# A mixture-of-experts kernel on one core: a finer table for the written order of its pieces, and a third buffer for sorted rows

## The reference

```
h = layernorm(x + o, g1, b1)
probs = softmax(h @ wg); topv, topi = top_k(probs, 2)
h1 = gelu(einsum('bsd,edf->ebsf', h, w1) + bb1)
y = einsum('ebsf,efd->ebsd', h1, w2) + bb2
moe = einsum('ebsd,bse->bsd', y, w)
return layernorm(h + moe, g2, b2)
```

## Time and profile before

| | |
|---|---|
| runs (3) | 1172.96, 1174.55, 1190.9 us; median 1174.55 |
| profiled execution, first to last instruction (its span) | 1192.8 us |
| its own time | not recorded beside the span; the span is 1.9 us above the longest of the three runs |
| instructions | 29724 |
| granted TensorE clock, mean | 0.898 |
| HBM traffic | 145.1 MB read, 38.7 MB written |

### The profile page before, as it was taken

One profiled execution on the slowest core, in us unless ns is written; L12 is line 12 of the kernel. 1 busy time (PEld: TensorE's weight loads), 2 busy tenths in 40 slices (PEclk: granted clock), 3 DMA queues, 4 the chain that ended last, 5 costly groups with the idle time before them and its releaser, 6 DMA issues. The chain is left out here.

```text
span 1192.8 us, 29724 instructions
## 1 busy us (share of the span) xinstructions
PE 1022.4 (86%) x10913; PEld 818.6 (69%) x10913; DVE 680.8 (57%) x2458; ACT 670.5 (56%) x1494; POOL 572.7 (48%) x693
## 2 busy tenths in 40 slices
PE   4799979998989989999989989998999988866470
PEld 2566656886877867686777867687777866766470
DVE  5657665655558835686568835686556723520314
ACT  1243424875758756675667757576666756534240
POOL 2223356235465455555565455554464456542515
PEclk9988877998999989898999979799999979887795
DMA  3394105555555545555556545555556545676562
GB/s 71 86 193 109 37 19 162 167 164 181 154 160 150 172 138 156 147 154 172 149 154 171 165 137 144 153 158 154 160 163 176 170 137 164 202 244 221 212 194 51
DMA packets 117239, 181.01 MB, mean 152 GB/s; under 512 B 13128, under 2 KB 80232, under 8 KB 117096
## 3 DMA queue, kind: packets, MB, share of 16 engines
q1 hardware_dynamic: 108904, 162.32, 47.7%
q0 software_dynamic: 8192, 16.79, 4.9%
HBM read 145.10 MB, written 38.68 MB: 154 GB/s over the span
## 5 line engine op out<-in xcount | busy, mean ns | idle before, releaser
L1173 POOL TENSOR_SCALAR_AFFINE_SELECT probs<-probs 128x512 f32<-128x512 f32 x256 | 182.5, 721 | 262.1 <-ACT probs L706 257.1
L706 ACT ACTIVATE probs<-ps_quad 128x768 f32<-128x768 f32 x256 | 193.7, 807 | 150.3 <-PE ps_quad L527 87.8
L744 ACT ACTIVATE act<-ps_ring,weights 128x128 f32<-128x128 f32 x696 | 191.8, 387 | 96.4 <-PE ps_ring L623 48.0
L874 DVE TENSOR_REDUCE shift_cols<-ps_quad 128x2 f32<-128x512 f32 (+3 forms) x256 | 149.9, 586 | 139.8 <-PE ps_quad L508 125.6
L632 PE MATMUL ps_ring<-weights,act 128*128 128x128 f32 x1392 | 190.8, 285 | 31.1 <-issue 16.4
L632 PEld LDWEIGHTS ps_ring<-weights,act 128*128 128x128 f32 x1392 | 174.5, 198 | 35.1 <-issue 21.6
L623 PE MATMUL ps_ring<-tile_t,weights 128*128 128x128 f32 x1392 | 187.6, 292 | 3.9 <-issue 3.2
L623 PEld LDWEIGHTS ps_ring<-tile_t,weights 128*128 128x128 f32 x1392 | 174.0, 204 | 16.8 <-issue 13.2
L1236 POOL DMA_INDIRECT picked<-sorted_outputs,place x128 | 123.7, 966 | 79.8 <-issue 78.6
L999 DVE TENSOR_TENSOR tile_y<-ps_ring,weights 128x128 f32<-128x128 f32 x174 | 48.8, 287 | 182.2 <-PE ps_ring L632 101.2
L1222 POOL DMA_INDIRECT sorted_rows<-h_rows,place x128 | 124.5, 972 | 53.5 <-issue 34.6
(11 more groups left out here) (165 smaller groups left out, 1531.5 us busy)
## 6 DMA issues: line engine op xcount, KB each, us to landing
weights<-expert_weights SPq DMA_DIRECT2D x174, 578.0 KB
tile_rows<-sorted_rows SPq DMA_DIRECT2D x56, 192.0 KB
sorted_outputs<-tile_y SPq DMA_DIRECT2D x56, 192.0 KB
query_key_parts<-qk SPq DMA_DIRECT2D x32, 256.0 KB, 5.0
k<-query_key_parts SPq DMA_DIRECT2D x64, 64.0 KB
q<-query_key_parts SPq DMA_DIRECT2D x64, 64.0 KB
sorted_rows<-zeros SPq DMA_DIRECT2D x2, 1472.0 KB, 10.7
xs<-in_L_attn_x SPq DMA_DIRECT2D x32, 64.0 KB, 2.3
```

Source lines behind the costliest of these rows:

```text
L706: sc.activation(probs[:, r % PROBS, 2 * a:2 * a + 2, :], ps_quad[:, 2 * a:2 * a + 2, 0:3 * P], ACT.Exp, scale=HD ** -0.5).then_inc(pair_fr ...
L744: ins = sc.activation(act[:, k % ACTS, f, :], bank(use)[:, f * P:(f + 1) * P], ACT.Gelu_apprx_tanh, bias=weights_of(k)[:, 2 * F + f:2 * F ...
L874: dve.tensor_reduce(shift_cols[:, late, groups], ps_quad[:, groups, 0:split], AX.X, ALU.max)
L1173: pool.affine_select(out=both, in_=both, compare_op=ALU.is_ge, fill=0.0, base=0, pattern=[[0, 2], [0, 2], [1, P]], channel_multiplier=-1). ...
```

## The change

1. `PLACES` holds a number for each kind of piece, for each of five stretches (set 0, set 1, sets 2 to 5, set 6, set 7) and, inside a set, for each turn (each sequence, job, row tile, batch or tile of the set). The numbers differ from the old ones mostly by tenths.
2. Sizes of sets may differ (`SET_SIZES`); all are 2, as before. Where sizes were constants there are functions now.
3. `DEPTH = 3`: three `sorted_rows`, `sorted_outputs`, `place` and `expert_at`, used in turn, with the waits for set s - 3 in place of s - 2, and three fills with zeros.

```diff
+SET_SIZES = (2, 2, 2, 2, 2, 2, 2, 2)
+DEPTH = 3
...
-    "scatter2": 12.578, "scatter3": 13.235, "load_tiles0": 13.754, "load_tiles": 12.816, "load_weights0": 13.277,
...
+    "exps0": ((0.263, 0.148, 0.021, 0.477), (0.283, 0.255, 0.363, 0.234), (0.399, 0.227, 0.334, 0.381),
+        (0.473, 0.228, 0.368, 0.356), (0.372, 0.24, 0.356, 0.169)),
...
+    "exps3": ((1.629, 1.758, 1.929, 2.013), (1.882, 1.617, 1.81, 1.881), (1.674, 1.722, 1.567, 1.822),
+        (1.834, 1.821, 1.794, 1.82), (1.826, 1.985, 1.818, 1.765)),
...
+    "scatter": ((12.159, 12.25, 12.394, 12.445, 12.758, 12.945, 13.288, 13.718),
+        (12.044, 12.325, 12.421, 12.604, 12.976, 13.002, 13.228, 13.358),
+        (11.675, 12.302, 12.614, 12.652, 12.931, 13.159, 13.355, 13.536),
+        (11.827, 12.226, 12.231, 12.665, 12.833, 13.182, 13.5, 13.582),
+        (11.087, 11.272, 11.391, 11.668, 12.614, 12.979, 13.089, 13.611)),
...
+def stretch_of(s):
+    return {0: 0, 1: 1, SETS - 2: 3, SETS - 1: 4}.get(s, 2)
...
-        for t in range(SET_TT):
-            put(8 * s, f"scatter{t // 2}", "scatter", s, t)
+        for t in range(SET_SIZES[s] * TT):
+            put(at, "scatter", "scatter", s, t)
...
+    def place(half, name, piece):
+        return half + PLACES[name][stretch_of(set_of(piece))][turn_of(piece)]
...
-                for i in range(2):
+                for i in range(DEPTH):
                     sp.dma_start(sorted_h[i].rearrange("(t p) d -> p t d", p=P),
                                  zeros[:, :].unsqueeze(1).broadcast_to([P, TILES, D])).then_inc(zeroed, 16)
...
-                if s >= 2:
-                    dve.wait_ge(combined, 2 * (s - 1))
...
+                if s >= DEPTH:
+                    dve.wait_ge(combined, FIRST_JOB[s - DEPTH + 1])
...
-                if s >= 2 and t == 0:
+                if s >= DEPTH and t == 0:
                     for par in range(2):
-                        pool.wait_ge(tile_y_out[par], 16 * (BATCHES // 2) * (s - 1))
...
+                        pool.wait_ge(tile_y_out[par], batches_stored(s - DEPTH, par))
```

More of the change, by code:

```diff
@@ L76, with set_of, turn_of @@
 }
+BY_SEQUENCE = ("scores", "exps", "weigh", "expand", "shift", "rows")
+BY_SET = ("rank", "scatter", "load_tiles", "turn_tiles", "store_tiles", "first", "second", "load_weights")
+def set_of(piece):
+    kind, no = piece[0], piece[1] if len(piece) > 1 else 0
+    if kind in BY_SET:
+        return no
+    return SET_OF[no // 2 if kind in BY_SEQUENCE else no + CHUNKS if kind == "store" else no]
+def turn_of(piece):
+    kind, no = piece[0], piece[1] if len(piece) > 1 else 0
+    if kind in BY_SET:
+        return 0 if kind == "rank" else piece[2]
+    if kind in BY_SEQUENCE:
+        return no - 2 * FIRST_JOB[set_of(piece)]
+    return (no + CHUNKS if kind == "store" else no) - FIRST_JOB[set_of(piece)]
+def stretch_of(s):
+    return {0: 0, 1: 1, SETS - 2: 3, SETS - 1: 4}.get(s, 2)
 def make_orders():
@@ L102, in make_orders @@
     for s in range(SETS):
-        put(8 * s, "rank", "rank", s)
-        for t in range(SET_TT):
-            put(8 * s, f"scatter{t // 2}", "scatter", s, t)
[L106 to L109, removed]
+        at = 4 * FIRST_JOB[s + 1] - 8
+        tiles_at = max(at, tiles_at + set_batches(s - 1)) if s else at
@@ L110, in make_orders @@
+        put(at, "rank", "rank", s)
+        for t in range(SET_SIZES[s] * TT):
+            put(at, "scatter", "scatter", s, t)
+        for q in range(set_batches(s)):
+            step = tiles_at + q
+            put(step, "load_tiles", "load_tiles", s, q)
+            put(step, "turn_tiles", "turn_tiles", s, q)
+            for t in batch_tiles(s, q):
                 if s == SETS - 1 and WEIGHTS <= t < WEIGHTS + SPARE:
-                    put(8 * s + 1 + 0.01 * (t - WEIGHTS + 1), "load_weights2", "load_weights", s, t)
+                    put(tiles_at + 1 + 0.01 * (t - WEIGHTS + 1), "load_weights", "load_weights", s, t)
@@ L112, in make_orders @@
                 else:
-                    put(8 * s + q, f"load_weights{n}", "load_weights", s, t)
+                    put(step, "load_weights", "load_weights", s, t)
                 for kind in ("first", "second"):
[L115 to L118, removed]
+                    put(step, kind, kind, s, t)
+            put(step, "store_tiles", "store_tiles", s, q)
@@ L119, in make_orders @@
+        for m in range(FIRST_JOB[s], FIRST_JOB[s + 1]):
+            c = m - FIRST_JOB[s]
+            done = tiles_at + set_batches(s) - 8
             for tt in range(TT):
-                put(8 * s + c, f"gather{tt}", "gather", m, tt)
+                put(done + c, f"gather{tt}", "gather", m, tt)
             for kind in ("combine", "end_norm", "end_norm_apply", "end_add"):
-                put(8 * s + c, kind, kind, m)
+                put(done + c, kind, kind, m)
             if m >= CHUNKS:
-                put(8 * s + c, "store", "store", m - CHUNKS)
+                put(done + c, "store", "store", m - CHUNKS)
@@ L125, in make_orders @@
             else:
                 for kind in ("long_norm", "long_norm_apply", "long_turn"):
-                    put(8 * s + 2 * c, kind, kind, m)
+                    put(done + 2 * c, kind, kind, m)
                 for b in range(2):
[L129 to L134, removed]
+                    put(done + 2 * c, f"long_scores{b}", "long_scores", m, b)
@@ L138, in make_orders @@
         own = [f for f in found if f[2][0] in kinds]
-        orders[engine] = [piece for _, _, piece in sorted(own, key=lambda f: place(engine, f[0], f[1]))]
+        orders[engine] = [piece for _, _, piece in sorted(own, key=lambda f: place(*f))]
     return orders
```

177 lines of the change are left out of this document (113 added, 64 removed), and 78 rows, old and new, of the table PLACES.

## The result

The changed kernel takes 1120.9 us (median of 4, 1118.1 to 1134.9) beside 1180.8 us before (median of 4, 1173.0 to 1190.9): ratio 0.948, 95% interval 0.940 to 0.957, so 5.2% less, where 2.8% was forecast. The ratio is taken without the changed kernel's longest run, whose granted clock was lower (0.911, the others 0.929 to 0.933). The profiled execution took 1118.9 us, with a span of 1117.2. That is near the median, while the span before, 1192.8 us, lies 12 us above its median: the two profiles are 75.6 us apart, the two medians 59.9 us.

The account below looks back on a forecast made before the run. TensorE was taken as the bound from 50 to 1000 us, slowed by unbroken DMA_INDIRECT runs; 49 - 8 - 5 = 36 us gained, 2 us lost: 1192.8 to 1159 profiled, ratio 0.972, so 1141 us; range 1106 to 1176.

Parts of the forecast that it names:

- about 5 us into an unbroken run: Claimed mechanism: that far into back-to-back DMA_INDIRECT on GpSimd, the other engines nearly stop until the run ends.
- the clock term: TensorE's half clock after stops: 3.2 us per set at most, half taken, 1.5 us times six sets, 9 us gain.
- the 40 us of second halves: Middle sets: time given back by splitting GpSimd's runs, 24 us from runs of eight and 16 us from runs of six.
- PE's busy time falls little: Sign expected in the profile after: PE stays about as busy while the span falls by some 35 us.
- New runs of four: Cost of the new runs of four DMAs in the sets: 0.25 us each, 8 us; upper end 39 us.
- The share that another engine doesn't follow: PE time won back but lost to the chain scores, exponentials, select, weigh: 5 us, without a row for it.
- The third buffer: Gain 0, since its waits never show; a third zero fill at the start costs 2 us, from 0 to 6.
- The tail: Last 130 us: long scatter and gather runs and their stops stay; change taken as 0, from -3 to +3 us.
- The stop doesn't end with the run: Rival: stops build up with DMA_INDIRECT count in some 20 us, selects don't clear them; 1168 us, chance 0.22.
- GpSimd has nothing to do with it: Rival: the pauses belong to PE's own stream at that place of the order; 1174 us, chance 0.08.
- More than the sum: Rival: clock stays up all set, the seventh run and ScalarE and VectorE steps count fully; 1108 us, chance 0.12.
- Slower: tiles come late: Rival: last scatters stand behind one more select, so PE waits for late tile rows; 1216 us, chance 0.08.

Follow-up runs that it names:

- b_gap: Kernel before, own order, two GpSimd scratch selects added after every four indirect DMAs of an unbroken run: 1130.4 us beside 1188.4 (0.950), chip 7.
- a_joined_2: Changed kernel with scatters and gathers alone back at the old numbers, runs of eight included, on chip 4: 1201.9 us, 1.001 of the kernel before.
- after_2: The changed kernel as it is, run again on chip 4: 1137.2 us, 0.948 of the kernel before there.
- The stream: Test kernel on chip 4: matmuls without waits beside GpSimd runs of sixteen DMAs, bare or with selects; unbroken scatters cut 48 matmuls per 5.1 us to 2.
- a_depth2: Changed kernel with two buffers in turn instead of three, on chip 12: 1013.4 us, 0.966 of the kernel before there.
- a_gap: Changed kernel with two buffers and two scratch selects after every four indirect DMAs, acting only on the tail, chip 7: 1105.8 us, 0.932 of before.
- the stream on chip 7: Wait-free matmul test kernel with other breaks and wide matmuls: one select per two DMAs keeps 48 or 49 matmuls per 5.1 us; a memset leaves 2.
- the wide matmuls: Phase of the chip 7 test kernel with PE alone and matmuls of 512 columns instead of 128 beside sixteen unbroken scatters: nothing lost.

## Why the prediction was right, and where it was off

*The mechanism* holds on chips 4 and 7 and, by the earlier trace rows, on that of the main comparison: unbroken runs of DMA_INDIRECT stop the other engines, breaking them gives the time back. b_gap shows it with the whole order fixed; a_joined_2 against after_2 shows it with the other engines' order fixed, but there the scatters and gathers also stand elsewhere. The prediction's "about 5 us into an unbroken run" had the right number for this kernel and the wrong quantity: what the stop follows is a count of instructions, and in the stretch of few and long ones there is none.

*The size* was too small: 36 us forecast for the order, 59.9 us measured by the medians (75.6 us between the two profiles), 64.7 and 58 us in the two experiments. The time, 1120.9 us, still lies in the range that was given, 1106 to 1176. The step that was sized wrong is the clock term, 9 us. It was taken from one stretch of 10 us at 0.68 as if that were all of a set's half clock, and then halved. The clock column over the long stretch stood in the earlier trace rows: 85.5 us short of full clock, 12.3 us for each of the 6.9 sets of 137 us, not 3.2. After the change it is 28.5 us, 57 us less; between a_joined_2 (0.92 over 1000 us) and after_2 (0.95 over 940 us) 80 - 47 = 33 us. Over the six sets of equal work it is 62 - 7 = 55 of the 71.9 us, and on chip 4 63 - 22 = 41 of 53.2 us. Some of it overlaps the stops themselves, so it isn't to be added to the 40 us of second halves; how the gain splits between the two isn't shown. But PE's idle time fell by 15.4 us only, and the clock is the only term large enough for the rest. The prediction's sign "PE's busy time falls little" failed by the same step: it fell by 64 us. The stream shows the same from the other side: 4.4 us are lost behind a run's own end, which halves of the run can't show.

*New runs of four*, 8 us: the right order. In the changed kernel there are 33 runs of four between 200 and 940 us. During the first, second, third and fourth DMA of a run (1.27 us each) PE begins 130, 93, 96 and 74 matmuls per 10 us. If the last place is thin by 32 against the mean of the others, that is 32 x 0.127 = 4.1 matmuls, 0.4 us a run, 13 us in all, an estimate. The same order on chip 12 (a_depth2) has 131, 113, 120 and 127, so that the last place isn't thin there. The sign "45 matmuls or more" holds in 31 of the 33 runs, the other two have 38 and 40, and no last 2.5 us are under 10. PE's idle time that no engine ended went from 44.7 us in 69 times to 22.0 us in 35 times; such pauses aren't gone.

*The share that another engine doesn't follow*, 5 us, was not tested.

*The third buffer*, 2 us, from 0 to 6: SyncE needs 12.40 us for three fills, not 7.08, 5.3 us more in place of 3.5, and PE's longest wait for query heads grew from 2.0 to 5.6 us. That growth isn't shown to come from the buffer: on chip 4 the longest such wait is 3.6 us with two buffers and 2.3 with three. In whole runs the price can't be seen. Its gain is 0, as said.

*The tail*, 0 from -3 to +3: measured +4.9 us. The run of fourteen gathers became sixteen and stops PE (5 and 8 matmuls in its second half, above); a_gap shows that in the new order the tail's runs are worth breaking up.

*The first set.* 8.2 us before set 0's first scatter were in no step. Nothing of the runs lies there; the order of the first stretch is new, and the clock from 120 to 160 us is 0.99, where the kernel before has 0.88. On chip 7 the first scatter comes at 163.5 us in b_gap, with the old order, and at 153.7 in a_gap, with the new one and as many buffers: that speaks for the order, by one execution each.

*The rivals.* "The stop doesn't end with the run" (1168) falls by b_gap and by the one select that is enough. "GpSimd has nothing to do with it" (1174) falls by the stream on chip 4 and by b_gap and the stream on chip 7. The Trainium skill's rule behind it (SBUF — State Buffer, "SBUF: two separate sides") isn't refuted as a rule on ports, since the wide matmuls read at full rate all through a run; it was wrong to take it for "GpSimd can't stop PE". "More than the sum" (1108) had the clock nearer, and its 20 us for it was too little too; as written it counts 9 us of clock twice, since the 49 us hold them. "Slower: tiles come late" (1216): PE's waits for tiles' rows are short.

```profile
PE ps_ring L796 <- ACT act L908: 28.8, 14, 13.8
PE ps_quad L657 <- ACT probs L870: 13.8, 18, 3.5
...
PE ps_ring L778 <- DMA tile_rows<-sorted_rows: 3.8, 3, 2.3
```

This is PE's list of waits in the changed kernel (us in total, times, the longest): three waits for rows, 2.3 us at most.

**What stays open.** Why chip 12 shows no stops, with the same durations of DMA_INDIRECT (0.96 us, 1.27 us from start to start). Chip 9 has the same time for the kernel before, but the one kernel traced there has no run over two. Whether the thing that fills up after some 175 instructions is the fetching of instructions, the recording of them or something else: every time here comes with a recorded span and clock, so no run could tell a kernel that is recorded from one that isn't. The Trainium skill has a rule that would fit (NOTIFIC — the notification-queue block, section "7.1 Overflow: three behaviours, one of which stalls the engine": inside the block that writes the records, a full stage holds up its producers rather than lose one); no run here shows it. And on chip 12 the changed order wins 3.4% with the runs split and 1.5% with them joined, while splitting alone loses 1.3%: why the two don't add up wasn't found. Where scatters and gathers stand is worth 22.5 us there without any stop (1035.9 against 1013.4, the latter with two buffers), so not all of chip 4's 64.7 us need be stops; b_gap's 58 us don't have this doubt.

## What to carry to other kernels

Read the granted clock over the longest stretch first, and multiply: (1 - clock) x length is the most that a cause that drops the clock can be worth, and one thin stretch isn't a bound on it. Don't let GpSimd issue more than four indirect DMAs without other work of 1.3 us (two selects) between them, and where the order can't be changed put an idle operation there: 1188 became 1130 us by that alone, though where a chip has no stops it may cost a per cent or two. Four aren't free: the bare stream still fell to 32 of 48 matmuls with two selects after every four, and lost none with one after every two. Before an order tuned on one chip is believed, it needs a run on another: the same change gave 0.948 in the main comparison and on chip 4, and 0.966 (with two buffers) on chip 12.

## What the runs showed of the hardware

- Two kinds of chips: the same kernel takes 1201.4 and 1188.4 us on chips 4 and 7 (1180.8 in the main comparison) and 1051.2 and 1055.1 us on chips 12 and 9. The mean granted clock of its runs is 0.89 to 0.91 on chips 4 and 7 and 0.94 to 0.96 on chips 12 and 9.
- On chips 4 and 7 a bare run of sixteen indirect DMAs (20 us) takes a stream of matmuls that waits for nothing from 48 to 2 or 3 per 5.1 us, and VectorE and ScalarE with it; on chip 12 it doesn't. It comes after 167 to 184 instructions, at 6 us with three engines busy and at 9 us with PE alone. 13 matmuls of 512 columns per 5.1 us go on undisturbed.
- One GpSimd select of 0.65 us after every two indirect DMAs ends it (chip 7); 0.14 us doesn't. Sixteen plain GpSimd DMAs in 8.6 us do nothing (chip 4).
- During a stop TensorE's granted clock falls to 0.50, 1.2 GHz, in the stream; 5 to 10 us behind the run's end it is at 1.00 again (0.50 in the first 5.1 us, 0.68 to 0.99 in the next).
